# A fused attention and mixture-of-experts block: layer-norm steps, a modulation chain and the first units' events moved in a hand-written order

## What is computed

```python
x = L0_attn_x                                   # (4, 512, 256)
mod = (silu(L0_c) @ L0_wmod).reshape(4, 6, 1, -1)
sa, ca, ga, sb, cb, gb = (mod[:, n] for n in range(6))
ga = (2 * (ga >= 0) - 1) * maximum(abs(ga), 0.25)      # gb alike
h = layernorm(x) * (1 + ca) + sa
x = x + ga * attention(h)      # 16 heads of 128, scores masked, softmax, W_O
h = layernorm(x) * (1 + cb) + sb
x = x + gb * experts(h)        # 8 experts, top 2, a shared expert, a core path
```

## Time and profile before

| | before |
|---|---|
| runs, median (lowest to highest) | 800.54 us (799.82 to 801.06), 3 runs |
| the profiled execution's own time | 800.14 us |
| its span, first to last instruction | 798.2 us |
| mean granted clock of TensorE | 0.993 of full speed |
| busy: PE, DVE, ACT, POOL | 776.1, 662.0, 624.9, 462.6 us |

### The profile page before, as it was taken

How to read it: one execution, slowest core, us unless ns; L and a number is a source line. 1 busy time by engine, 2 the same in 40 slices (tenths; PEclk the granted TensorE clock), 3 DMA queues, 4 the chain that set the end, 5 groups by cost and what they waited for, 6 DMA issues and landing times.

```text
span 798.2 us, 14365 instructions
## 1 busy us (share of the span) xinstructions
PE 776.1 (97%) x4700; PEld 690.7 (87%) x4700; DVE 662.0 (83%) x1649; ACT 624.9 (78%) x1449; POOL 462.6 (58%) x389
## 2 busy tenths in 40 slices
PE   8899999999999999999999999999999899989997
PEld 7689989999999999999999999999999677768786
DVE  4779998878888878888878888879898988786967
ACT  3787889877777888777888877887879868866974
POOL 2454456765557666555576655575445365677654
PEclk8999999999999999999999999999999999999999
DMA  7252233442223444223343332344222131112231
GB/s 250 83 171 69 67 93 96 113 105 67 67 67 71 101 111 120 70 67 70 84 106 93 93 93 69 85 110 133 69 67 67 48 119 55 53 41 68 75 98 53
DMA packets 47593, 70.53 MB, mean 88 GB/s; under 512 B 5536, under 2 KB 38464, under 8 KB 47392
## 3 DMA queue, kind: packets, MB, share of 16 engines
q1 hardware_dynamic: 47008, 68.81, 32.9%
q0 software_dynamic: 368, 0.81, 0.3%
q10 hardware_dynamic: 144, 0.00, 0.0%
HBM read 25.49 MB, written 2.17 MB: 35 GB/s over the span
## 4 chain that ended last, share of the span: by engine, by line
PE 79%; ACT 8%; DVE 7%; issue 3%; POOL 2%; DMA 1%; SPq 0%; DVEq 0%; POOLq 0%
PE M L759 12%; PE M L760 12%; PE M L758 12%; PE T L758 8%; PE T L760 8%; PE T L759 8%; PE S L758 5%; PE S L760 5%; PE S L759 5%; PE M L864 2%; ACT PB L696 1%; ACT PB L647 1%; PE S L849 1%; POOL stage L565 1%; DMA PB<-in_wmod 1%
## 5 line engine op out<-in xcount | busy, mean ns | idle before, releaser
L604 POOL TENSOR_TENSOR ptl<-ptl,pth 128x896 fp32r<-128x896 f32 x126 | 179.7, 1448 | 94.7 <-ACT pth L726 94.7
L696 ACT ACTIVATE PB<-PB,ri 128x256 f32<-128x256 f32 (+3 forms) x256 | 123.2, 553 | 30.4 <-DVE ri L1180 30.3
L647 ACT ACTIVATE PB<-S,nb 128x128 f32<-128x128 f32 (+3 forms) x256 | 135.2, 540 | 7.1 <-DVE nb L1171 6.9
L1160 DVE TENSOR_TENSOR qk<-M,qk 128x512 fp32r<-128x512 f32 x108 | 74.2, 687 | 58.8 <-ACT qk L711 58.7
L592 POOL TENSOR_TENSOR X<-X,fb 128x512 f32<-128x512 f32 x64 | 83.2, 1300 | 61.1 <-DVE fb L1207 61.0
L1171 DVE CUSTOM_DVE_ANT_0 S<-S,cc 128x128 f32<-128x128 f32 (+3 forms) x256 | 117.3, 520 | 1.3 <-PE S L760 1.3
L711 ACT CAST qk<-M 128x512 fp32r<-128x512 f32 x108 | 64.3, 595 | 67.0 <-PE M L760 67.0
L1187 DVE STREAM_TRANSPOSE gab<-PB 128x256 f32<-128x256 f32 (+2 forms) x192 | 109.5, 624 | 6.7 <-DMA ptl<-gab 2.2
L760 PE MATMUL M<-hh,W 128*128 128x512 f32 x222 | 87.5, 394 | 0.0
L759 PE MATMUL M<-hl,W 128*128 128x512 f32 x222 | 87.3, 393 | 0.0
L758 PE MATMUL M<-hh,W 128*128 128x512 f32 x222 | 86.8, 391 | 0.5 <-DVE hl L1146 0.5
(11 more groups left out here) (264 smaller groups left out, 2491.8 us busy)
## 6 DMA issues: line engine op xcount, KB each, us to landing
ptl<-gab SPq DMA_DIRECT2D x256, 160.0 KB, 3.1
stage<-in_wat SPq DMA_DIRECT2D x16, 512.0 KB, 5.1
gab<-scw SPq DMA_DIRECT2D x16, 256.0 KB, 3.2
tmp<-scw SPq DMA_DIRECT2D x16, 256.0 KB, 3.4
X<-in_x SPq DMA_DIRECT2D x3, 512.0 KB, 8.2
stage<-in_wfa SPq DMA_DIRECT2D x3, 512.0 KB, 4.8
out<-X SPq DMA_DIRECT2D x3, 512.0 KB, 2.6
X<-in_wmod SPq DMA_DIRECT2D x1, 1024.0 KB, 12.1
```

The lines of the kernel that those rows point to most:

```text
L604: pool.tensor_tensor(pt_part(lo, c), pt_part(lo, c).bitcast(F32), pt_part(hi, c).bitcast(F32), ALU.subtract).then_inc(s_pl, 1)
L647: ins = act.activation(PB[:, P_OFF[i]:P_OFF[i] + w], PS[bk][:, a:a + w], ACT.Exp, bias=nb[:, i:i + 1], scale=-1.0, accum_out=sm[:, i:i + 1])
L696: act.activation(p, p, ACT.Copy, scale=ri[:, i:i + 1]).then_inc(s_P3, 1)
L1160: v.tensor_tensor(lo, src, hi.bitcast(F32), ALU.subtract).then_inc(me, 1)
```

## The change

It reorders events. No instruction that computes anything is added or removed.

1. `nm` of batches 2 and 3 and of the two second norms in the attention: two empty groups are put ahead of its two halves, so that they follow the third and fourth of the events named above (`wo` and `v`) in place of the first and second (`S` and `q`).
2. `h` of batch 1 moves from iteration 0's end (ahead of and behind `z` of unit 0) to behind `S` of unit 2 and behind `ty` of unit 2.
3. `mg` moves from behind `v` of pair 0 to behind `pt` of unit 0, and `mh` behind `wh` 3. `v` of pair 0, first half, moves ahead of `nm` of batch 1. `ri` of unit 1 moves behind `k` of unit 2, `v`'s second half ahead of `pt` of unit 0.
4. The exponentials of units 1 and 2 take the order that the later units have; before, unit 1's began ahead of ACT's part of `q` of unit 2.

```diff
--- before.py
+++ after.py
@@ -57,11 +57,11 @@
     for b in (1, 2, 3):
         i = (0, 2, 5)[b - 1]
         if b == 1:
-            put(pre, i, ("h", b, 0))
-            put(post, i, ("h", b, 1))
+            put(mid, (i, 0), ("h", b, 0))
+            put(mid, (i, 1), ("h", b, 1))
             continue
         fill[i] = [[("st", b, 0)], [("st", b, 1)], [("st", b, 2)], [("st", b, 3)]]
-        fill[i + 1] = [[("nm", b, 0)], [("nm", b, 1)]]
+        fill[i + 1] = [[], [], [("nm", b, 0)], [("nm", b, 1)]]
         put(mid, (i + 2, 0), ("h", b, 0))
         put(mid, (i + 2, 1), ("h", b, 1))
     for n in range(4, 16):
@@ -70,7 +70,7 @@
         put(pre, 34 + n, ("wh", n))
     for b in range(2):
         fill[54 + 4 * b] = [[("st", B + b, k)] for k in range(4)]
-        fill[55 + 4 * b] = [[("nm", B + b, 0)], [("nm", B + b, 1)]]
+        fill[55 + 4 * b] = [[], [], [("nm", B + b, 0)], [("nm", B + b, 1)]]
         put(mid, (56 + 4 * b, 0), ("h2", b, 0))
         put(mid, (56 + 4 * b, 1), ("h2", b, 1))
     put(post, 60, ("wh", 20))
@@ -78,9 +78,9 @@
         ("silu",), ("nb", 0), ("nm", 0, 0), ("nm", 0, 1), ("mod",), ("wh", 0), ("ld", 2),
         ("h", 0, 0), ("h", 0, 1), ("wh", 1), ("ld", 3),
         ("q", 0), ("st", 1, 0), ("st", 1, 1), ("k", 0), ("wh", 2), ("ld", 4), ("S", 0), ("st", 1, 2), ("st", 1, 3),
-        ("q", 1), ("ri", 0), ("k", 1), ("norm", 0), ("nb", 1), ("ty", 0), ("nm", 1, 0), ("nm", 1, 1), ("v", 0, 0),
-        ("mg",), ("tr", 0), ("S", 1), ("q", 2), ("ri", 1), ("k", 2), ("norm", 1), ("ty", 1), ("pt", 0), ("mh",), ("v", 0, 1),
-        ("wh", 3), ("tr", 1)]
+        ("q", 1), ("ri", 0), ("k", 1), ("norm", 0), ("nb", 1), ("ty", 0), ("v", 0, 0), ("nm", 1, 0), ("nm", 1, 1),
+        ("tr", 0), ("S", 1), ("q", 2), ("k", 2), ("ri", 1), ("norm", 1), ("ty", 1), ("v", 0, 1), ("pt", 0), ("mg",),
+        ("wh", 3), ("mh",), ("tr", 1)]
     loads = {0: [5]}
     for i, events in pre.items():
         for ev in events:
@@ -710,12 +710,11 @@
                         src = bank(ev)[:, 0:256]
                     act.copy(dst, src).then_inc(mh, 1)
                     if kind == "q" and ev[1] >= 2:
-                        exps(ev[1] - 1, [1, 2] if ev[1] == 2 else [0, 1])
-                    if kind == "k" and ev[1] >= 3:
+                        exps(ev[1] - 1, [0, 1])
+                    if kind == "k" and ev[1] >= 2:
                         exps(ev[1] - 1, [2])
-                elif kind == "ex" or kind == "S" and ev[1] < 2:
-                    u = ev[1]
-                    exps(u, [0] if u == 1 else [0, 1, 2])
+                elif kind == "ex" or ev == ("S", 0):
+                    exps(ev[1], [0, 1, 2])
                 elif kind == "ra":
                     act.wait_ge(s_rt, 3)
                     act.activation(rt[:, 64:96], rt[:, 32:64], ACT.Exp).then_inc(s_ra, 1)
```

## The result

| | before | after |
|---|---|---|
| runs, median (lowest to highest) | 800.18 us (797.93 to 801.06), 4 runs | 809.25 us (807.14 to 809.91), 4 runs |
| profiled execution, its span | 800.14, 798.2 us | 808.73, 806.6 us |
| mean granted clock of TensorE | 0.993 | 0.992 |

The ratio is 1.0113, interval 1.0091 to 1.0135: the change makes the kernel slower by 1.1%. The forecast was 806.4 us with a range up to 808.3; the direction was right, and the time lies 0.95 us beyond the range.

A forecast was written before the change was run, and what follows sets the result against it. PE, busy 97% of the span, was taken as the bound, so only its waits could move the time. Terms -1.6 + 2.5 + 1.0 + 4.3 = +6.2 us on 800.14 us gave 806.3, stated as 806.4 us; range 798.8 to 808.3 us.

The forecast's parts named there:

- Second norms: Iterations 55 and 59: PE waits 2.15 us at each `h2` for `nm`, held up by POOL; +4.3 us together.
- Batch 2: Iteration 3: PE comes to `h` at 77.2 us, ready at 79.7, and waits 2.5 us for `nm`; +2.5 us.
- batch 3: Iteration 6: the 1.20 us wait at the scores goes, but `h` comes 1.9 us later; net +1.0 us.
- The prologue: Start to `z` of unit 1: 3.0 us of PE waits go, a new 1.4 us wait comes; -1.6 us.
- `h` itself waits for no bank: Prologue, batch 1's moved `h`: its bank's last user, five events earlier, is evacuated some microseconds before.
- the 1.4 us at `z`: Unit 1: PE waits 1.4 us for POOL's first piece; without it PE would only wait longer at batch 2's `h`.
- The sum: Whole kernel: the terms -1.6, +2.5, +1.0 and +4.3 make +6.2 us, forecast as 806.4 us.
- everything that makes PE wait is paid in full: From 54 to 106 and 108 to 600 us PE is always busy, so any wait there adds to the time.
- A: The forecast, with `nm` held by POOL: +6.2 us, 806.4 us, own range 804 to 808.5; chance 0.66, 0.03 for more.
- B: Rival: POOL does not collide with DVE's `nm`; -0.6 us, 799.7 us; chance 0.17.
- C: Rival: ACT and DVE run ahead, both `nm` halves are done before PE asks; -2.8 us, 797.5 us; chance 0.11.
- D: Rival: the moved events change nothing PE sees, new waits equal the old; 800.1 us; chance 0.03.

The follow-up runs named there:

- pool_short: Changed kernel with POOL's subtractions of units 4, 7, 56, 60 cut to 16 columns, its additions to X there to 4: 800.06 us, ratio 1.0003.
- mg_early: Changed kernel with `mg` moved behind `st` of batch 1, ahead of `q` of unit 1: 810.28 us, ratio 1.0141.
- fill: Changed kernel with 32 idle PE products of 128 columns ahead of the `nm` wait at each of four first transposes: 805.66 us, ratio 1.0053.
- pro_only: Changed kernel with `nm` where it was before (parts 2 to 4 alone): 797.32 us, ratio 0.9960; repeat 797.20 us, ratio 0.9956.
- nm_only: Kernel before with part 1 of the change alone (`nm` behind `wo` and `v`): 811.66 us, ratio 1.0148.
- both_wo: Changed kernel with both halves of `nm` behind `wo`, ahead of the transposes of `ty`: 797.16 us, ratio 0.9962; repeat 797.09 us, ratio 0.9961.
- e2: Changed kernel with `mg` early, `nm` of batch 3 behind `wo`, the other three `nm` where they were before the change: 798.75 us, ratio 0.9989.
- fill_mid: both_wo with 52 idle PE products in the wait at 711 us, ahead of the third batch's first expert product: 796.24 us, ratio 0.9959.
- e1: both_wo with `mg` early as in mg_early: 798.54 us, ratio 0.9981.

## Why the prediction was right in its steps and short in its sum

- **Second norms, +4.3 us from waits.** Right: 2.08 and 2.10 us where 2.15 each was worked out, with the points of the chain compared above within 0.2 us. `pool_short` shows the split that the prediction gave: 0.57 and 0.55 us from the order (0.5 forecast), 1.5 from POOL. The Trainium skill ("SBUF — State Buffer", "Who interferes with whom") says that where a `tensor_scalar` of DVE takes the ports that it shares with GpSimd, the later of the two to issue is blocked for the whole of the other's instruction. The trace agrees: the 1.71 us of two instructions become 0.73 when POOL's are short.
- **Batch 2, +2.5, and batch 3, +1.0 net.** The mechanism right: waits of 2.08 us, and of 2.31 less 1.20 us. That batch 2 is 0.4 us short and the prologue 0.55 us less gain is one error, not two: what PE does not gain in the prologue it does not wait at `h`.
- **The prologue, -1.6 us.** The mechanism right, the size off: -1.05 us. The wait at `z` of unit 1 was 1.34 us (1.4 forecast). What was left out stands behind the sentence that `h` itself waits for no bank: that is so, but `z` of unit 0, five events on, takes the bank of batch 1's first `h` and waited 0.60 us for its evacuation. The forecast looked at the bank that `h` needs and not at the one that it passes on.
- **That the 1.4 us at `z` cost nothing by themselves.** Borne out by `mg_early`: without them PE waits 1.2 us longer at `h`, and the time is no less, though new waits of 1.0 us at the scores blur the test.
- **The sum, +6.2 us.** Its waits make 8.57 - 1.20 - 1.05 = +6.3 us in the trace, and the median rose by 9.1 us. The step that failed is "everything that makes PE wait is paid in full", as if the wait were the whole price: the sum puts the clock behind a wait at nothing, and gives no reason. It came to 3.2 us in the profiled execution, 3.0 us between the stretches of `fill` and of the changed kernel, and 3.6 us between their medians. Rows for it were in the trace of before, at 712 us, where the clock falls to half behind a wait of 3.05 us. Beside this the base is a little low: 6.2 us on the median of 800.54 us are 806.7, not 806.4 us, and the upper end of the range, 808.3 us, lies below the 808.5 of its own A. The time fell where the forecast had left a chance of 0.03.
- **Rivals.** B (no meeting with POOL, 799.7 us) is close to what `pool_short` builds, 800.1 us, though that keeps one meeting at batch 3. So its price was good and its condition untrue. C did not happen: ACT's cast follows PE, as argued. D is excluded.

## What to carry to other kernels

Where one engine is busy throughout, ask of each moved instruction when the engine that is the bound will want its result, and count on that path what the other engines do at the same time, above all POOL under DVE's `tensor_scalar`. A wait of 2 us on TensorE can cost more than 2 us, since the clock may fall behind it: here each fall cost 1.4 to 1.8 us, and two of four waits had one, 0.8 us for each wait in the mean. And a gain ahead of a wait that another engine sets is worth nothing until that wait is gone: here the 3 us of parts 2 to 4 could be kept by leaving `nm` alone (`pro_only`, 797.2 us).

## What the runs showed of the hardware

The granted clock falls to half behind some waits of 2.1 us and not behind others of the same length: in the changed kernel behind two of four, in `nm_only`, with waits of 2.71, 2.40, 2.09 and 2.08 us, behind the first two, in `mg_early`, with 3.27, 2.49, 2.09 and 2.08 us, behind all but the longest. So the length of the wait alone does not decide, and what does is open. The clock then stays at half for 3 to 4 us. In three profiles (`both_wo`, `e2`, `fill_mid`) it also falls at 682 to 684 us, behind no wait over 0.3 us. Time and clock also go together from run to run: the fastest of the 23 runs of before in one series took 797.86 us at a mean clock of 0.996, the slowest 803.01 us at 0.991. DVE's `tensor_scalar` of 128x256 took 0.36 us alone and up to 1.87 us under an instruction of POOL, and one `tensor_tensor` of that size took 0.41 us before and 2.01 us after the change, beside POOL's pieces; three transposes of DVE took 1.7 us with and without POOL. With so much scatter, differences under 1.5 us, such as `e1` against `both_wo`, stay open.
